# A recommender tower on one core: half-sums on GpSimd between gathers, transposes only when a stage is due

## The chip, the cores and the metric

One core of a Trainium2 chip runs the kernel. The metric is the device time in microseconds, lower is better. The core has a matrix engine (TensorE, PE in the profile), a vector engine (VectorE, DVE), an activation engine (ScalarE, ACT), a general one that here issues the gathers (GpSimd, POOL), and a queue engine for ordinary transfers (SyncE, SP). They work beside each other and meet only through semaphores.

## What is computed

All data are float32. For 2048 rows of a batch, 32 tables give one embedding of 64 numbers each; every pair of embeddings is combined through its own 64x64 matrix, and a small network follows:

```python
e = jnp.stack([tbl_0[ids[:, 0]], ..., tbl_31[ids[:, 31]]], axis=1)   # 2048 x 32 x 64
II, JJ = np.triu_indices(32, k=1)                                   # 496 pairs
z = jnp.sum(e, axis=-1)                                             # 2048 x 32
outer = jnp.einsum('bpd,pde,bpe->bp', e[:, II], kernels, e[:, JJ])  # 2048 x 496
h = jnp.concatenate([z, outer, dense_ctx], axis=1)                  # 2048 x 544
h = jnp.maximum(h @ W_top1 + b_top1, 0.0)                           # 512
h = jnp.maximum(h @ W_top2 + b_top2, 0.0)                           # 256
y = h @ W_top3                                                      # 1
```

## The kernel before

**Tiling.** The batch is cut into `NQ` = 4 quarters of `QB` = 512 rows, a quarter into 4 tiles of 128 rows. The 32 tables are taken in 16 pairs, the stages a = 0 to 15. A stage needs 8 gathers (4 tiles, 2 tables), each of 128 rows of 64 numbers into `gathered`, which has `GR` = 4 stage buffers. TensorE transposes a stage (`transpose`, line 322, four instructions into the one bank `tr`), and ScalarE copies it to `x_t` (`keep_x`, line 207), where the embeddings of two tables lie on 128 partitions with the batch along the row.

**Products.** The pair matrices stay in `k_sb`, loaded once in ten transfers, as 128 doubles; a double takes stage a against an earlier stage. Stage a brings a doubles, one more where a is odd, so the early stages bring few and the late ones many: the first double of stage a is number 0, 0, 2, 4, 8, 12, 18, 24, 32, 40, 50, 60, 72, 84, 98, 112 (`FIRST`). For each double TensorE makes two matmuls into one of `MR` = 3 pieces of `m_ps` (`multiply`, lines 386 and 387), VectorE multiplies 128x1024 results with `x_t` (`product`, line 300) into one of 7 buffers `prod`, and TensorE sums them over partitions with small selecting matrices into `acc` (`reduce`, line 398). Four doubles are a group g; a quarter has 32 groups, and the reduce of a group follows the products of the next. [...]

**Sums and layers.** The sum of each embedding is made by VectorE from `gathered` (`sum_x`, line 287, one reduction of 512 numbers to 8 for each partition and stage) into `z_nat`; TensorE turns it (piece "s"). The three layers of quarter q-1 (pieces "h1", four of them, "h2", two, and "y") are put between the groups of quarter q, after groups 1, 3, 5, 7, then 9, 11 and 13. Those of the last quarter stand at the end.

**The order** is written out by hand in two tables, `BEFORE` and `AFTER`, of what is done ahead of the products of a group and behind its reduce; all engines walk them in the same order (`ORDER`), since all pieces share the bank `tr`. In the first quarter stage a stands ahead of group `min(FIRST[a] // 4 - (a > 5), (4 a - 7) // 3)`, in later ones behind group 18 + 2a of the quarter before (`group_of_stage`, line 62), so that its transposes run on into group 16 of its own quarter.

**GpSimd** issues the 512 gathers in order (line 176), at most four in flight. The first gather of a stage waits for the transpose (`tr_filled`) and VectorE's sum (`x_summed`) of the stage four before it; in later quarters gather n of a stage also waits for VectorE's product 4 (g - 3) + n, g the group of its transpose, which spreads the gathers, one for each product:

```python
pool.wait_ge(prod_ready, GROUP * (group_of_stage(q, a) - 3) + n)
```

## Time and profile before

| | |
|---|---|
| median of 3 runs | 1015.3 us (1012.37 to 1015.33) |
| the profiled execution | 1018.13 us, its span 1016.3 us |
| mean granted clock of TensorE in it | 0.963 of full |
| TensorE busy | 886.5 us (87%) |
| VectorE busy | 641.3 us (63%) |
| GpSimd busy | 483.6 us (48%) |
| ScalarE busy | 69.3 us (7%) |

The profile is of one execution. Its busy times are unions of recorded spans; the ends of matmuls are modelled. A row of the timeline gives start, duration, engine, line, operation, what is written from what, and in brackets how long the engine sat idle before and who released it. "issue" is idle time with no releaser in the profile, "remote" one whose releaser is not recorded; some matmul records are missing.

### The profile page before, as it was taken

To read this page: it belongs to the slowest core of one execution; us is meant where nothing else is said; L and a number is where in the kernel's file an instruction comes from. 1 tells how busy PE (TensorE), PEld (TensorE's weight loads), DVE (VectorE), ACT (ScalarE), POOL (GpSimd) and SP (SyncE) were. 2 spreads that over 40 slices of the span, in tenths; PEclk is the share of its full clock that TensorE was granted. 3 is DMA by queue.
4 is the path that set the end of the run, shared out by engine and by line. 5 is a ranking of instruction groups with operands and counts; after the bars stand their busy time and mean duration, and the time that the engine had idled before them with its cause. 6 is when DMAs were issued, how large, how long until landed. Compare 5 with 4: busy or idle time off the path is not lost.

```text
span 1016.3 us, 11896 instructions
## 1 busy us (share of the span) xinstructions
PE 886.5 (87%) x4608; PEld 311.6 (31%) x4608; DVE 641.3 (63%) x579; ACT 69.3 (7%) x113; POOL 483.6 (48%) x518
## 2 busy tenths in 40 slices
PE   0323579699999999998999999998999999999998
PEld 0111123223333333333333333323333333333333
DVE  0102257578887575687877656676787657688850
ACT  0000000000000001000000101000000101000001
POOL 5774735536565444555666444554556445400000
PEclk9956779999999999999999999999999999999999
DMA  9310101101111000110111010011101000000000
GB/s 348 107 27 15 27 14 19 21 12 23 23 21 23 17 17 18 20 21 20 22 23 22 15 19 17 19 22 19 21 19 24 15 17 19 19 1 1 1 1 0
DMA packets 19777, 28.20 MB, mean 28 GB/s; under 512 B 8901, under 2 KB 9413, under 8 KB 18825
## 3 DMA queue, kind: packets, MB, share of 16 engines
q0 software_dynamic: 16384, 16.81, 8.6%
q1 hardware_dynamic: 3336, 10.63, 2.9%
q8 instruction: 37, 0.61, 0.3%
q14 instruction: 20, 0.16, 0.1%
HBM read 27.40 MB, written 0.01 MB: 27 GB/s over the span
## 4 chain that ended last, share of the span: by engine, by line
PE 77%; another core or an unknown queue 8%; issue 7%; DVE 4%; DMA 2%; ACT 1%; SPq 1%; POOL 1%; DVEq 0%; POOLq 0%
PE m_ps L386 39%; PE acc L398 21%; PE tr L341 4%; DVE prod L300 3%; PE tr L328 3%; PE tr L347 2%; PE m_ps L387 2%; DMA w_sb<-in_w 2%; PE m_ps L341 1%; PE tr L339 1%; PE m_ps L347 1%; PE tr L353 1%; POOL gathered L176 1%; SPq L186 1%
## 5 line engine op out<-in xcount | busy, mean ns | idle before, releaser
L300 DVE TENSOR_TENSOR prod<-m_ps,x_t 128x1024 f32<-128x1024 f32 x512 | 604.3, 1219 | 302.5 <-PE m_ps L387 180.7
L176 POOL DMA_INDIRECT gathered<-in_tbl,idx x512 | 482.9, 943 | 403.4 <-DVE prod L300 178.2
L386 PE MATMUL m_ps<-x_t,k_sb 64*128 64x512 f32 x1024 | 501.4, 623 | 74.6 <-DVE prod L300 35.6
L387 PE MATMUL m_ps<-x_t,k_sb 64*128 64x512 f32 x1024 | 502.3, 624 | 0.0
L386 PEld LDWEIGHTS m_ps<-x_t,k_sb 64*128 64x128 f32 x1024 | 180.7, 191 | 346.9 <-issue 261.6
L398 PE MATMUL acc<-prod,sel 128*32 128x512 f32 x2048 | 247.0, 600 | 0.0
L387 PEld LDWEIGHTS m_ps<-x_t,k_sb 64*128 64x128 f32 x1024 | 180.6, 191 | 0.0
L398 PEld LDWEIGHTS acc<-prod,sel 128*32 128x32 f32 x2048 | 53.7, 109 | 176.5 <-issue 119.6
L328 PE MATMUL tr<-ident,gathered 128*128 128x128 f32 x256 | 44.5, 299 | 50.6 <-DMA gathered<-in_tbl,idx 41.4
L213 ACT ACTIVATE x_t<-tr 128x512 f32<-128x512 f32 x64 | 38.2, 597 | 471.7 <-PE tr L328 275.3
L287 DVE TENSOR_REDUCE z_nat<-gathered 128x8 f32<-128x512 f32 x64 | 43.1, 675 | 38.1 <-DMA gathered<-in_tbl,idx 38.1
L328 PEld LDWEIGHTS tr<-ident,gathered 128*128 128x128 f32 x256 | 28.5, 147 | 100.7 <-issue 87.4
L341 PE MATMUL tr<-z_sb,w_sb 128*128 128x512 f32 x96 | 44.4, 605 | 0.0
L341 PEld LDWEIGHTS tr<-z_sb,w_sb 128*128 128x128 f32 x96 | 17.2, 189 | 26.3 <-issue 26.3
L247 ACT ACTIVATE z_sb<-acc 128x512 f32<-128x512 f32 x16 | 9.6, 597 | 202.4 <-PE acc L398 129.5
L347 PE MATMUL tr<-h_sb,w_sb 128*128 128x512 f32 x48 | 22.2, 605 | 0.0
L217 ACT ACTIVATE h_sb<-tr,b_sb 128x512 f32<-128x512 f32 x12 | 8.2, 687 | 112.3 <-PE tr L341 112.3
L341 PE MATMUL m_ps<-z_sb,w_sb 128*128 128x512 f32 x32 | 14.8, 605 | 0.0
L339 PE MATMUL tr<-z_sb,w_sb 48*128 48x512 f32 x24 | 13.5, 641 | 0.0
L347 PEld LDWEIGHTS tr<-h_sb,w_sb 128*128 128x128 f32 x48 | 8.6, 189 | 13.6 <-issue 13.6
L341 PEld LDWEIGHTS m_ps<-z_sb,w_sb 128*128 128x128 f32 x32 | 5.8, 189 | 8.8 <-issue 8.8
L353 PE MATMUL tr<-h_sb,w_sb 128*1 128x512 f32 x16 | 7.5, 592 | 0.8 <-ACT h_sb L268 0.8
(24 smaller groups left out, 39.6 us busy)
## 6 DMA issues: line engine op xcount, KB each, us to landing
gathered<-in_tbl,idx POOLq DMA_INDIRECT x512
k_sb<-in_kmat SPq DMA_DIRECT2D x7, 1024.0 KB, 14.3
w_sb<-in_w SPq DMA_DIRECT2D x1, 1280.0 KB
k_sb<-in_kmat SPq DMA_DIRECT2D x2, 256.0 KB, 4.2
k_sb<-in_kmat SPq DMA_DIRECT2D x1, 512.0 KB, 6.4
w_sb<-in_w SPq DMA_DIRECT2D x1, 512.0 KB
idx<-in_ids SPq DMA_DIRECT2D x1, 256.0 KB, 2.7
z_sb<-in_dense_t SPq DMA_DIRECT2D x4, 32.0 KB
```

Of the source, the lines that this page charges most:

```text
L176: nc.gpsimd.indirect_dma_start(out=gathered[:, G % GR, t, f, :], out_offset=None, in_=tables[2 * (STAGES - 1 - a) + f], in_offset=bass.Ind ...
L213: nc.scalar.activation(x_t[:, q % 2, a, :], tr[:], ACT.Copy).then_inc(tr_kept, 1)
L287: nc.vector.tensor_reduce(z_nat[:, q % 2, :, 2 * a:2 * a + 2], gathered[:, G % GR, :, :, :], axis=AX.X, op=ALU.add).then_inc(x_summed, 1)
L300: nc.vector.tensor_tensor(prod[:, p % PR, :, :], m_ps[:, p % MR, :, :], other, ALU.mult).then_inc(prod_ready, 1)
L328: last = nc.tensor.transpose(tr[:, t * P:(t + 1) * P], gathered[:, G % GR, t, :, :].rearrange("p f d -> p (f d)"), ident[:])
L339: nc.tensor.matmul(to, w1_sb[0:ZLAST, NB, n * P:(n + 1) * P], z_sb[0:ZLAST, NB, :], start=True, stop=False)
L341: last = nc.tensor.matmul(to, w1_sb[:, b, n * P:(n + 1) * P], z_sb[:, b, :], start=False, stop=(b == NB - 1))
L347: last = nc.tensor.matmul(to, w2_sb[:, c, n * P:(n + 1) * P], h1_sb[:, c, :], start=(c == 0), stop=(c == H1 // P - 1))
L353: last = nc.tensor.matmul(to, w3_sb[:, c:c + 1], h2_sb[:, c, :], start=(c == 0), stop=(c == H2 // P - 1))
L386: nc.tensor.matmul(m_ps[:, p % MR, 0, :], k_sb[0:D, d, :], x_t[0:D, q % 2, a0, :], start=True, stop=True)
L387: nc.tensor.matmul(m_ps[:, p % MR, 1, :], k_sb[D:P, d, :], x_t[D:P, q % 2, a1, :], start=True, stop=True).then_inc(unit_done, 1)
L398: last = nc.tensor.matmul(acc[c * 32:c * 32 + 32, :], sel[:, 30 - 2 * row:62 - 2 * row], prod[:, (q * ND + 2 * n + c // 2) % PR, c % 2, :] ...
```

## The change

GpSimd adds the two halves (32 and 32 numbers) of every gathered embedding into a new buffer `x_fold` of four stages: it is given 512 additions, each between two gathers, of the gather issued four earlier (`fold_x`). VectorE's reduction reads `x_fold`, 256 numbers for each partition, and has its own table `SUM_AT`: it stands where the next stage is due, that of stage 15 ahead of group 29. A gather no longer waits for a product; the first of a stage waits for the transpose four stages before, and the first addition of a stage waits for VectorE's sum four stages before. In the first quarter a stage stands ahead of group `FIRST[a] // 4 - (a > 8)`, in later ones behind the group just ahead of its first product, stages 0 and 1 behind groups 28 and 30 of the quarter before. The turned sums move to group 30. To make room in memory, `y_sb` becomes a part of `h2_sb`, and with it the wait for the store of y moves to the first eviction of h2.

```diff
--- before.py
+++ after.py
@@ -61,11 +61,11 @@
 
 def group_of_stage(q, a):
 
-    return 18 + 32 * (q - 1) + 2 * a
+    return min(NG * q - 4 + 2 * a, NG * q + FIRST[a] // GROUP - 1)
 
 
 for _a in range(STAGES):
-    _g = 0 if _a < 3 else min(FIRST[_a] // GROUP - (_a > 5), (4 * _a - 7) // 3)
+    _g = FIRST[_a] // GROUP - (_a > 8)
     BEFORE.setdefault((0, _g), []).append(("x", 0, _a))
 for _q in range(1, NQ):
     for _n in range(H1 // P):
@@ -75,8 +75,15 @@
     AFTER.setdefault((_q, 13), []).append(("y", _q - 1, 0))
     for _a in range(STAGES):
         AFTER.setdefault(divmod(group_of_stage(_q, _a), NG), []).append(("x", _q, _a))
-    AFTER.setdefault((_q, 18), []).append(("s", _q, 0))
-AFTER.setdefault((0, NG - 1), []).append(("s", 0, 0))
+    AFTER.setdefault((_q, 30), []).append(("s", _q, 0))
+AFTER.setdefault((0, 30), []).insert(0, ("s", 0, 0))
+
+
+SUM_AT = {}
+for _q in range(NQ):
+    for _a in range(STAGES):
+        _g = NG * _q + 29 if _a == STAGES - 1 else FIRST[_a + 1] // GROUP if _q == 0 else group_of_stage(_q, _a + 1) + 1
+        SUM_AT.setdefault(divmod(_g, NG), []).append((_q, _a))
 ORDER = [e for q in range(NQ) for g in range(NG) for e in BEFORE.get((q, g), []) + AFTER.get((q, g), [])]
 PLACE = {e: n for n, e in enumerate(ORDER)}
 
@@ -100,6 +107,7 @@
         k_sb = sb("k_sb", [P, ND, P])
         x_t = sb("x_t", [P, 2, STAGES, QB])
         gathered = sb("gathered", [P, GR, TILES, 2, D])
+        x_fold = sb("x_fold", [P, GR, TILES, 2, D // 2])
         prod = sb("prod", [P, PR, 2, QB])
         z_sb = sb("z_sb", [P, NB + 1, QB])
         z_nat = sb("z_nat", [P, 2, TILES, SUM_ROWS])
@@ -158,25 +167,32 @@
             nc.gpsimd.affine_select(out=ident[:], in_=ident[:], compare_op=ALU.not_equal, fill=1.0,
                                     base=0, pattern=[[-1, P]], channel_multiplier=1).then_inc(consts_ready, 1)
             pool.wait_ge(idx_loaded, 16)
-            for G in range(NQ * STAGES):
+            def fold_x(k):
+                G, n = divmod(k, GATHERS)
                 q, a = divmod(G, STAGES)
-                if G >= GR:
+                t, f = divmod(n, 2)
+                pool.wait_ge(gather_landed[k % IN_FLIGHT], (k // IN_FLIGHT + 1) * 16)
+                if n == 0 and G >= GR:
+                    pool.wait_ge(x_summed, G - GR + 1)
+                nc.gpsimd.tensor_tensor(x_fold[:, G % GR, t, f, :], gathered[:, G % GR, t, f, 0:D // 2],
+                                        gathered[:, G % GR, t, f, D // 2:D], ALU.add).then_inc(x_folded, 1)
+
+            for k in range(NQ * STAGES * GATHERS):
+                G, n = divmod(k, GATHERS)
+                q, a = divmod(G, STAGES)
+                t, f = divmod(n, 2)
+                if k >= IN_FLIGHT:
+                    fold_x(k - IN_FLIGHT)
+                if n == 0 and G >= GR:
                     pool.wait_ge(tr_filled, place("x", *divmod(G - GR, STAGES)))
-                    pool.wait_ge(x_summed, G - GR + 1)
-                for n in range(GATHERS):
-                    t, f = divmod(n, 2)
-                    if q:
-
-                        pool.wait_ge(prod_ready, GROUP * (group_of_stage(q, a) - 3) + n)
-                    k = G * GATHERS + n
-                    if k >= IN_FLIGHT:
-
-                        pool.wait_ge(gather_landed[k % IN_FLIGHT], k // IN_FLIGHT * 16)
-                    col = ((q * STAGES + a) * 2 + f) * TILES + t
-                    nc.gpsimd.indirect_dma_start(
-                        out=gathered[:, G % GR, t, f, :], out_offset=None, in_=tables[2 * (STAGES - 1 - a) + f],
-                        in_offset=bass.IndirectOffsetOnAxis(ap=idx[:, col:col + 1], axis=0),
-                    ).then_inc(gather_landed[k % IN_FLIGHT], 16)
+                    pool.wait_ge(x_folded, (G - GR + 1) * GATHERS)
+                col = ((q * STAGES + a) * 2 + f) * TILES + t
+                nc.gpsimd.indirect_dma_start(
+                    out=gathered[:, G % GR, t, f, :], out_offset=None, in_=tables[2 * (STAGES - 1 - a) + f],
+                    in_offset=bass.IndirectOffsetOnAxis(ap=idx[:, col:col + 1], axis=0),
+                ).then_inc(gather_landed[k % IN_FLIGHT], 16)
+            for k in range(NQ * STAGES * GATHERS - IN_FLIGHT, NQ * STAGES * GATHERS):
+                fold_x(k)
 
         @block.sync
         def _(sp):
...
@@ -218,13 +234,13 @@
 
             def keep_h2(q, n):
                 act.wait_ge(tr_filled, place("h2", q, n))
+                if q and n == 0:
+                    act.wait_ge(y_stored, 16 * q)
                 nc.scalar.activation(h2_sb[:, n, :], tr[:], ACT.Relu, bias=b2_sb[:, n:n + 1]).then_inc(tr_kept, 1)
 
             def keep_y(q):
                 act.wait_ge(tr_filled, place("y", q, 0))
-                if q:
-                    act.wait_ge(y_stored, 16 * q)
-                nc.scalar.activation(y_sb[:], tr[0:1, :], ACT.Copy).then_inc(tr_kept, 1)
+                nc.scalar.activation(y_sb, tr[0:1, :], ACT.Copy).then_inc(tr_kept, 1)
 
             def keep_sums(q):
                 act.wait_ge(tr_filled, place("s", q, 0))
...
@@ -277,16 +293,6 @@
             dve.wait_ge(sel_zeroed, 1)
             nc.vector.memset(sel[0:D, 30:31], 1.0).then_inc(consts_ready, 1)
             nc.vector.memset(sel[D:P, 31:32], 1.0).then_inc(consts_ready, 1)
-            def sum_x(q, a):
-                G = q * STAGES + a
-                for landed in gather_landed:
-                    dve.wait_ge(landed, (G + 1) * GATHERS // IN_FLIGHT * 16)
-                if q >= 2 and a == 0:
-
-                    dve.wait_ge(tr_filled, place("s", q - 2, 0))
-                nc.vector.tensor_reduce(z_nat[:, q % 2, :, 2 * a:2 * a + 2], gathered[:, G % GR, :, :, :],
-                                        axis=AX.X, op=ALU.add).then_inc(x_summed, 1)
-
             def product(q, d):
                 p, (_, _, u0, u1) = q * ND + d, DOUBLES[d]
                 dve.wait_ge(unit_done, p + 1)
@@ -299,16 +305,21 @@
                     other = x_t[:, q % 2, u0:u1 + 1, :]
                 nc.vector.tensor_tensor(prod[:, p % PR, :, :], m_ps[:, p % MR, :, :], other, ALU.mult).then_inc(prod_ready, 1)
 
+            def sum_x(q, a):
+                G = q * STAGES + a
+                dve.wait_ge(x_folded, (G + 1) * GATHERS)
+                if q >= 2 and a == 0:
+
+                    dve.wait_ge(tr_filled, place("s", q - 2, 0))
+                nc.vector.tensor_reduce(z_nat[:, q % 2, :, 2 * a:2 * a + 2], x_fold[:, G % GR, :, :, :],
+                                        axis=AX.X, op=ALU.add).then_inc(x_summed, 1)
+
             for q in range(NQ):
                 for g in range(NG):
-                    for what, h, n in BEFORE.get((q, g), ()):
-                        if what == "x":
-                            sum_x(h, n)
+                    for h, a in SUM_AT.get((q, g), ()):
+                        sum_x(h, a)
                     for d in range(GROUP * g, GROUP * (g + 1)):
                         product(q, d)
-                    for what, h, n in AFTER.get((q, g), ()):
-                        if what == "x":
-                            sum_x(h, n)
 
         @block.tensor
         def _(pe):
```

GpSimd in the second quarter. Ahead of the change, the gathers of a stage:

```order
L176 DMA gathered<-in_tbl,idx 128x64 [waits gather_landed3,prod_ready]
L176 DMA gathered<-in_tbl,idx 128x64 [waits prod_ready,gather_landed0,x_summed,tr_filled]
L176 DMA gathered<-in_tbl,idx 128x64 [waits gather_landed1,prod_ready]
L176 DMA gathered<-in_tbl,idx 128x64 [waits gather_landed2,prod_ready]
L176 DMA gathered<-in_tbl,idx 128x64 [waits gather_landed3,prod_ready]
```

and with it:

```order
L177 TENSOR_TENSOR x_fold<-gathered 128x32 [waits gather_landed0]
L190 DMA gathered<-in_tbl,idx 128x64 [waits x_folded,tr_filled]
L177 TENSOR_TENSOR x_fold<-gathered 128x32 [waits gather_landed1]
L190 DMA gathered<-in_tbl,idx 128x64
L177 TENSOR_TENSOR x_fold<-gathered 128x32 [waits gather_landed2]
L190 DMA gathered<-in_tbl,idx 128x64
L177 TENSOR_TENSOR x_fold<-gathered 128x32 [waits gather_landed3]
L190 DMA gathered<-in_tbl,idx 128x64
L177 TENSOR_TENSOR x_fold<-gathered 128x32 [waits x_summed,gather_landed0]
```

An addition stands ahead of each gather and holds the wait for the landing; the wait for a product is gone, and the one for VectorE's sum has moved four gathers on, to the stage's first addition.

TensorE in the first quarter, behind the reduce of group 1. Ahead of the change, stages 5 and 6 are transposed together ahead of group 3 (`tr` from `gathered`):

```order
L398 MATMUL acc<-prod,sel 32x512 x3
L328 MATMUL tr<-ident,gathered 128x128 [waits gather_landed3,gather_landed2,tr_kept,gather_landed1,gather_landed0]
L328 MATMUL tr<-ident,gathered 128x128 x3
L328 MATMUL tr<-ident,gathered 128x128 [waits gather_landed3,gather_landed2,tr_kept,gather_landed1,gather_landed0]
L328 MATMUL tr<-ident,gathered 128x128 x3
L386 MATMUL m_ps<-x_t,k_sb 128x512 [waits prod_ready,tr_kept,k_loaded2]
```

and with it, at the same place and behind the next reduce:

```order
L409 MATMUL acc<-prod,sel 32x512 x3
L339 MATMUL tr<-ident,gathered 128x128 [waits gather_landed3,gather_landed2,tr_kept,gather_landed1,gather_landed0]
L339 MATMUL tr<-ident,gathered 128x128 x3
L397 MATMUL m_ps<-x_t,k_sb 128x512 [waits prod_ready,tr_kept,k_loaded2]
```

Stage 6 has moved behind the four products of group 3, ahead of group 4, whose third product is its first.

VectorE in the first quarter. Ahead of the change (sums `z_nat`, products `prod`):

```order
L287 TENSOR_REDUCE z_nat<-gathered 128x4x2 [waits gather_landed2,gather_landed3,gather_landed1,gather_landed0] x2
L300 TENSOR_TENSOR prod<-m_ps,x_t 128x1024 [waits reduced,unit_done] x8
L287 TENSOR_REDUCE z_nat<-gathered 128x4x2 [waits gather_landed2,gather_landed3,gather_landed1,gather_landed0]
L300 TENSOR_TENSOR prod<-m_ps,x_t 128x1024 [waits reduced,unit_done] x8
```

and with it:

```order
L314 TENSOR_REDUCE z_nat<-x_fold 128x4x2 [waits x_folded]
L306 TENSOR_TENSOR prod<-m_ps,x_t 128x1024 [waits reduced,unit_done] x4
L314 TENSOR_REDUCE z_nat<-x_fold 128x4x2 [waits x_folded]
L306 TENSOR_TENSOR prod<-m_ps,x_t 128x1024 [waits reduced,unit_done] x8
```

A sum now waits for GpSimd's additions of its stage, and stands where the next stage's first product is due.

## Rows read from the trace of the kernel before

**Rows 1.** The page, busy us, share of the span, instructions of each engine.

```profile
PE 886.5 (87%) x4608; PEld 311.6 (31%) x4608; DVE 641.3 (63%) x579; ACT 69.3 (7%) x113; POOL 483.6 (48%) x518
```

**Rows 2.** Stretches of 25 us: busy time (and instructions) of each engine, clock, DMA.

```profile
core 0: us, PE busy (x) PEld busy (x) DVE busy (x) ACT busy (x) POOL busy (x), PEclk, DMA share, GB/s
50.00:75.00 25.00, 6.55 (x16) 2.75 (x16) 2.02 (x3) 0.60 (x1) 18.90 (x21) 0.52 0.14 27
...
100.00:125.00 25.00, 15.99 (x72) 5.46 (x68) 8.10 (x8) 1.19 (x2) 18.74 (x21) 0.77 0.13 26
125.00:150.00 25.00, 16.58 (x76) 5.52 (x76) 13.00 (x12) 0.60 (x1) 9.21 (x11) 0.73 0.07 14
150.00:175.00 25.00, 22.26 (x130) 7.58 (x132) 19.57 (x18) 1.68 (x3) 12.92 (x14) 1.00 0.10 19
...
500.00:525.00 25.00, 23.97 (x140) 8.01 (x136) 19.88 (x19) 1.79 (x3) 15.08 (x16) 1.00 0.12 22
```

**Rows 3.** The chain that ended last, in order of time: start, duration, what.

```profile
334.29 3.63 PE tr L341 x8
...
557.78 3.63 PE tr L341 x8
...
785.53 3.63 PE tr L341 x8
...
936.49 1.85 PE acc L398 x16
941.98 1.85 PE acc L398 x16
...
980.40 3.62 PE acc L398 x32
```

**Rows 4.** Groups of instructions: form and count, busy us and mean ns, idle before.

```profile
L328 PE MATMUL tr<-ident,gathered 128*128 128x128 f32 x256 | 44.5, 299 | 50.6 <-DMA gathered<-in_tbl,idx 41.4 <-ACT x_t L213 4.8 <-ACT z_sb L231 4.5
L287 DVE TENSOR_REDUCE z_nat<-gathered 128x8 f32<-128x512 f32 x64 | 43.1, 675 | 38.1 <-DMA gathered<-in_tbl,idx 38.1
```

**Rows 5.** Timeline of GpSimd at the start: start us, duration us, instruction.

```profile
0.25 0.10 POOL L470 MEMSET const-float32-0.0<- 128x1 f32 x1 [0.25 <-issue]
...
1.19 0.28 POOL L158 TENSOR_SCALAR_AFFINE_SELECT ident<-ident 128x128 f32<-128x128 f32 x1 [0.24 <-POOL ident L156]
3.73 1.10 POOL L176 DMA_INDIRECT gathered<-in_tbl,idx  x1 [2.26 <-DMA idx<-in_ids]
...
38.11 0.94 POOL L176 DMA_INDIRECT gathered<-in_tbl,idx  x1 [0.30 <-issue]
```

**Rows 6.** Timeline of the first quarter, 41 to 98 us, all engines.

```profile
41.74 1.22 PE L386 MATMUL m_ps<-x_t,k_sb 64*128 64x512 f32 x1
...
50.67 1.09 PE L328 MATMUL tr<-ident,gathered 128*128 128x128 f32 x4 [2.85 <-DMA gathered<-in_tbl,idx]
...
67.88 0.60 ACT L213 ACTIVATE x_t<-tr 128x512 f32<-128x512 f32 x1 [25.43 <-issue]
...
68.57 1.19 PE L386 MATMUL m_ps<-x_t,k_sb 64*128 64x512 f32 x1 [16.81 <-issue]
...
79.78 1.23 DVE L300 TENSOR_TENSOR prod<-m_ps,x_t 128x1024 f32<-128x1024 f32 x1 [21.28 <-remote]
...
88.04 0.94 POOL L176 DMA_INDIRECT gathered<-in_tbl,idx  x1 [0.30 <-issue]
...
96.84 0.60 ACT L213 ACTIVATE x_t<-tr 128x512 f32<-128x512 f32 x1 [28.37 <-remote]
```

**Rows 7.** Timeline, two later ends of unbroken gathers and what followed.

```profile
128.46 0.94 POOL L176 DMA_INDIRECT gathered<-in_tbl,idx  x1 [0.30 <-issue]
...
133.56 4.71 DVE L300 TENSOR_TENSOR prod<-m_ps,x_t 128x1024 f32<-128x1024 f32 x4 [4.54 <-remote]
...
165.26 0.94 POOL L176 DMA_INDIRECT gathered<-in_tbl,idx  x1 [0.30 <-issue]
...
167.96 1.23 DVE L300 TENSOR_TENSOR prod<-m_ps,x_t 128x1024 f32<-128x1024 f32 x1 [2.46 <-remote]
```

11 lines of the change are left out of this document (6 added, 5 removed).

## The prediction

> **What bounds the kernel now.** I read the busy times first [rows 1]: TensorE is busy for 886.5 us of a span of 1016.3 us (87%), VectorE for 641.3, GpSimd for 483.6. So some 130 us of the span are not TensorE's, and the question is where they lie. The table by stretches [rows 2] answers it: in the stretches from 50, 100 and 125 us TensorE is busy 6.55, 15.99 and 16.58 us of 25, and its granted clock is 0.52 to 0.77; from 500 us it is busy 23.97 of 25 at full clock. The tail after the last reduce, which ends at 984 [rows 3], is the layers of the last quarter, and this change leaves it alone.
>
> Where TensorE is full, a group of four products costs 5.49 us: two reduces in the chain of work stand at 936.49 and 941.98 [rows 3]. A quarter of the batch is 32 groups, 175.7 us; its 16 transposes add 11 (44.5 us for 64 of them, 0.70 each [rows 4]), its layers 27: eight matmul records of L341 take 3.63 [rows 3], a layer-1 part has ten, so 4.54, and there are four; two layer-2 parts have eight, and layer 3 four, 1.8. That is 214 us. The first layer-1 matmuls of successive quarters stand at 334.29, 557.78 and 785.53 [rows 3], 223 and 228 us apart: later quarters lie only 9 to 14 us over their floor. The first one starts its products at 41.7 us [rows 6] and should need 32 groups (176), 19 transposes (13) and two more groups (11), so layer 1 could start at about 242; it starts at 334. **Ninety us are lost in the first quarter**, and they are what this change can win.
>
> Why are they lost? GpSimd issues a gather every 1.25 us there: 0.94 busy and 0.30 in front [rows 5, 6]. A stage is eight gathers, 10 us, so the gathers of 16 stages could be done by 4 + 160 = 164 us, and for the first five groups TensorE does wait for data. But the timeline [rows 6] shows something else as well. The transpose of stage 3 ran at 50.67 to 51.76, and ScalarE, with nothing else to do, evicted it only at 67.88. Products that TensorE started at 68.57 were taken by VectorE at 79.78. What TensorE signals arrives late, while what ScalarE and VectorE signal is acted on at once (67.88 + 0.60 is followed by TensorE at 68.57). It is released when GpSimd pauses: the gathers stop at 88.98, and ScalarE goes on at 96.84; they stop at 129.40, and VectorE is free at 133.56; in a short burst they stop at 166.20, and VectorE goes on at 167.96 [rows 6, 7]. Over the lengths of these bursts (56, 30 and 10 us) the arrears of 7.9, 4.2 and, less a usual 0.3, 1.4 us are all near 14%. So I take it that a gather in an unbroken row leaves 1.25 x 1.14 = 1.42 us of something that delays TensorE's signals, and that nothing piles up when gathers stand 1.42 us apart or more. In later quarters, where a gather waits for each product, they come 16 in 25 us, 1.6 us apart [rows 2], and TensorE is full. This is an inference; its cause in the hardware I cannot name.
>
> **The change part by part.** *The fold on GpSimd*: 512 additions of 128x32. No row shows one. The nearest are the affine select of 128x128 at 0.28 us, with 0.24 us of idle time in front, and a set of 128x1 at 0.10 us [rows 5]. Lower bound 0.10 with no gap of its own (cadence 1.35), upper bound 0.28 plus a gap of 0.30 (cadence 1.83). I take 0.17 plus 0.08, nearer to the 128x1 row since a fold has 32 elements for each partition, so a gather every **1.50 us**; it waits for no landing, since the gather it reads was issued four gathers (6 us) earlier, and in the trace of before, where four gathers are 5.0 us, the idle time is the plain 0.30 [rows 5, 6]. On GpSimd this adds 512 x 0.25 = 128 us to 484 busy, on an engine idle for over half the span: it is hidden, except where gathers are the bound.
>
> The Trainium skill (GPSIMD Engine Reference, Performance versus the Vector engine) says that a two-input elementwise instruction on GpSimd costs about 2.6 cycles for each element and speaks against putting it there; for 32 elements that would be an estimate of 0.07 us beyond the dispatch. No run here shows it, and by it alone the cadence would stay near 1.4 and the time near the lower end of my range.
>
> *Start-up*: TensorE's first product needs stage 2, 24 gathers. The first starts at 3.73 and the 24th at 38.11 [rows 5], 1.49 us apart on average, since some are held by landings while the loads run; 20 folds at 0.25 put it 5 us later at most, so products start at 45 instead of 41.7.
>
> *The first quarter's new order*: a stage is transposed one group or less before its first product; stages 5 and 6 are no longer both wanted in group 3, and stages 10 to 15 are wanted in groups 11, 14, 17, 20, 23 and 27 instead of 11, 12, 13, 15, 16 and 17. With 8 x 1.50 + 0.2 = 12.2 us for a stage, stage a is there at 45 + 12.2 x (a - 2): stage 6 at 94, stage 8 at 118, stage 10 at 143, stage 15 at 204. If TensorE's signals are prompt, it waits for stages 3 to 10 (groups 0 to 10), and from group 11 it is the bound: 21 groups at 5.49 are 115, nine transposes and one set of sums 7, so the first quarter ends at 143 + 122 = 265 and layer 1 begins two groups later, at 277. While it waits TensorE is busy for about half the time, so the granted clock will be at its lower level as from 50 us now [rows 2]; a group at 1.2 GHz, some 10 us (2.4 GHz gives 5.49), is still under the 12.2 of a stage, but groups 4 to 10 lose some; I add 3 to 6. Layer 1 at 282 to 283 against 334.29: **minus 51 us**.
>
> *VectorE's sums*: the reduction reads 256 elements for each partition instead of 512. It took 0.675 us for 512 [rows 4]; a product of 1024 takes 1.23 [rows 6], so an element is near 1 ns, and it saves about 0.27 us x 64 = 17 us of VectorE, which is not the bound (4 x 1.23 of 5.49 us in a group). Where the sum delays a product that TensorE waits for, some of it is won: minus 0 to 8, I take 4.
>
> *No pacing in later quarters*: a gather no longer waits for a product. It is held by four buffers: gather 0 of a stage by the transpose four stages back, and the fold in front of gather 4 by VectorE's sum four stages back. So a stage comes as four and four, or eight in a row, and then a pause. *Stages wanted close together*: at a quarter's end stages 2 to 6 are transposed after groups 31 to 35. From the moment when VectorE has summed stage 15 (group 29), 24 gathers lie between it and the landing of stage 5, 32 for stage 6. In time, groups 29 to 34 last 5.5, 6.8, 6.1, 6.1, 10.7 (with a layer-1 part) and 6.1: stage 5 is wanted 41 us after it, stage 6 52 us after. Gathers at 1.50 bring them at 36 + 2.1 and 48 + 2.1, just in time; at 1.83, at 46 and 61, so 5 and then 4 us late, three times. I take plus 2 for each of three ends: plus 6. The other edits (sums after group 30, y written over h2, waits for the store of y that ended a quarter before) have time behind other work: nothing, and if the store were late, 2 us of ScalarE.
>
> Sum: -51 - 4 + 6 = **-49 us**. From the profiled execution, 1018.1 us (span 1016.3), that gives 969; the median of the runs shown is 1015.3, and so **966 us**.
>
> **The rivals.** *TensorE's signals stay late.* For it: the folds may not thin out what delays them (if the 1.42 us is work of GpSimd's own, a fold adds to it, and 1.42 + 0.17 is more than 1.50), and the pauses of the later quarters are gone. The first quarter would then crawl as now, in runs of gathers ended by the four buffers: gain 0 to 20. The later quarters would look like 142 to 200 us now, where bursts of eight end with a signal 1.8 us late at 166 and TensorE lacks 2.7 us of 25 [rows 2, 7]; 48 stages at 1.2 to 1.5 us are 58 to 72. Time: 1015 - 20 + 50 = **1045**, between 1015 and 1075. It decides from a cadence under the 1.42 us, or a rate of arrears that grows with the fold. Against it: 1.6 us apart there is no trace of it.
>
> *The fold is dear (cadence 1.8 or more).* Stage 15 would come at 48 + 13 x 14.8 = 240, the first quarter would end at 295 (gain 24), and three ends would cost 9 each: 1015 - 24 + 27 = **1018**, no change.
>
> *The waits of the first quarter cost more*: TensorE cold until group 14 and stages at 13.5 us each: layer 1 at 300, **985 to 1000**.
>
> *Better than the sum*: cadence 1.38 and prompt signals let stage 10 come at 133, and the later quarters come nearer to their floor: 1015 - 61 - 15 = **940 to 950**.
>
> **How the numbers follow.** My sum, with a cadence of 1.42 to 1.65 (950 to 982): 0.52. Costly waits (983 to 1000): 0.12. Better than 950: 0.09. Dear fold (about 1018): 0.07, of which 0.04 is within 0.3% (1012 to 1018, about what a measurement of this kernel can tell from no change) and 0.03 slower. Late signals: 0.20, of which 0.02 faster, 0.02 the same and 0.16 slower. So faster 0.75, same 0.06, slower 0.19. The range leaves out most of the part under 950 and the upper half of the late signals: 948 to 1042.
>
> **What would show it.** GpSimd's gathers in the first 100 us 1.4 to 1.6 us apart and the fold 0.10 to 0.28 us; ScalarE's eviction of each transpose within 1 us of it; layer 1 of the first quarter at 275 to 295; TensorE 24 to 25 us busy in each 25 from 200 us on, also at the ends of quarters. Wrong: evictions 5 us or more after their transposes while gathers run, gathers over 1.8 us apart, or TensorE at 20 to 22 in 25 all through.

## The result, and the profile after

The changed kernel takes 1073.45 us (median of 3 runs, 1072.43 to 1076.22) where the kernel before takes 1015.3: 1.059 times as long, 95% interval 1.055 to 1.063. The forecast was 966 us and faster, so it was wrong in sign; the rival "TensorE's signals stay late" (1015 to 1075) is the one whose range holds it. The profiled execution has a span of 1070.6 us, against 1016.3.

One fact that the first two traces did not hold has to be told first, since everything after it rests on it. The experiments ran on five chips, and the same kernel before takes 931 to 935 us on three of them and 1010 to 1022 us on the other two. (Three of its runs are slow ones and left out: 1510 us at a granted clock of 0.57, 1105 us at 0.83, and one of 1026 us.) I call them **kind A** (934 us) and **kind B** (1015 us). The prediction and the result are of kind B. None of the five chips served for more than one set of experiments, so whether the kind belongs to the chip or to the hour is not shown; "chip" below means the set that ran on it. The changed kernel is slower on both: 1.036 times (1.034 to 1.038) on kind A.

The page's first part, busy times of the changed kernel, beside [rows 1]:

```profile
PE 895.0 (84%) x4608; PEld 320.6 (30%) x4608; DVE 626.4 (59%) x579; ACT 70.2 (7%) x113; POOL 626.6 (59%) x1030
```

TensorE is now idle for 176 us of the span, before for 130. VectorE has lost 15 us of work and GpSimd has won 143, but neither bounds the kernel. The stretches of 25 us of the changed kernel, columns as in [rows 2]:

```profile
50.00:75.00 25.00, 14.56 (x56) 6.38 (x56) 8.80 (x10) 1.19 (x2) 21.95 (x36) 0.73 0.12 24
100.00:125.00 25.00, 7.89 (x30) 2.02 (x32) 5.23 (x5) 0.60 (x1) 21.82 (x36) 0.59 0.12 24
275.00:300.00 25.00, 17.45 (x92) 6.56 (x86) 10.08 (x10) 1.18 (x2) 21.19 (x35) 0.86 0.13 24
325.00:350.00 25.00, 14.09 (x56) 5.33 (x49) 6.78 (x7) 1.28 (x2) 21.81 (x36) 0.80 0.12 24
550.00:575.00 25.00, 16.54 (x66) 6.44 (x60) 7.45 (x8) 2.48 (x4) 21.84 (x37) 0.87 0.12 24
800.00:825.00 25.00, 17.74 (x60) 6.91 (x62) 7.67 (x7) 2.48 (x4) 21.83 (x36) 0.80 0.12 24
```

From 50 us TensorE is busy for twice the time that it was before (14.56 against 6.55 of 25), from 100 us for half of it (7.89 against 15.99): the first quarter is better in parts only. New are the holes at the ends of the quarters, at 275, 325, 550 and 800 us, where TensorE falls to 14 to 18 of 25 and its clock to 0.80 to 0.87. In every one of them GpSimd is busy for 21 to 22 of 25, which means gathers and folds without a break.

The first matmul of layer 1 of each quarter but the last (it answers to [rows 3]) shows how the 54 us between the two spans are spread. Timeline of TensorE in the changed kernel (start us, duration us; x2 are the two records that the trace has of this one matmul, as it has 1024 at one line for its 512 products):

```profile
313.06 1.12 PE L350 MATMUL tr<-z_sb,w_sb 48*128 48x512 f32 x2
...
562.04 1.12 PE L350 MATMUL tr<-z_sb,w_sb 48*128 48x512 f32 x2
...
809.85 1.12 PE L350 MATMUL tr<-z_sb,w_sb 48*128 48x512 f32 x2
```

I use the same instruction as a mark in all kernels. The table gives where it first stands, the two distances to the next ones, and the rest to the end of the span, in us, from each kernel's own timeline:

| kernel (kind of chip) | first mark | quarter | quarter | rest | span |
|---|---|---|---|---|---|
| before (B) | 333.2 | 223.5 | 227.7 | 231.9 | 1016.3 |
| changed (B) | 313.1 | 249.0 | 247.8 | 260.7 | 1070.6 |
| e5 before (A) | 272.9 | 214.1 | 214.1 | 231.7 | 932.7 |
| e6 changed (A) | 266.7 | 226.3 | 226.3 | 245.8 | 965.2 |
| e1 no gathers in quarters 2 to 4 (A) | 268.4 | 225.9 | 225.9 | 245.5 | 965.7 |
| e8 new order alone (A) | 257.3 | 226.3 | 226.3 | 245.7 | 955.7 |
| e2 every fold twice (A) | 293.3 | 237.5 | 226.3 | 245.8 | 1002.9 |
| e7 one group earlier (A) | 265.7 | 221.8 | 215.8 | 235.5 | 938.7 |
| e14 folds alone (A) | 288.5 | 214.1 | 214.1 | 231.9 | 948.5 |
| e16 first quarter's order alone (A) | 257.2 | 230.6 | 214.1 | 231.7 | 933.6 |
| e18 folds alone (B) | 320.5 | 219.5 | 219.4 | 232.0 | 991.3 |
| e9 first quarter's order alone (B) | 348.9 | 267.1 | 225.3 | 232.3 | 1073.6 |
| e11 new order one group earlier (B) | 356.7 | 249.8 | 252.9 | 248.7 | 1108.0 |
| e12 no spacing of gathers (B) | 370.1 | 237.0 | 235.5 | 231.7 | 1074.3 |
| e10 layers moved (B) | 314.2 | 244.4 | 232.4 | 255.0 | 1046.0 |
| e17 one group earlier, spaced (B) | 330.4 | 240.4 | 245.8 | 235.9 | 1052.5 |

The rows of kind B come from different chips, and these differ by some us: the kernel before has a median of 1015.3, 1014.5 and 1018.6 us on three of them, and only the first has its trace. A difference of two B rows holds to some us only.

The changed kernel on kind B: 20 us won before the first mark, then 25.5, 20.1 and 28.8 lost. The kernel before is itself not at its best there: its three later parts take 683.1 us, and 659.9 on kind A. The floor of 214 us that the prediction worked out for a quarter is what kind A measures (214.1).

What the prediction said of single instructions can be read in the groups and in GpSimd's timeline of the changed kernel:

```profile
L177 POOL TENSOR_TENSOR x_fold<-gathered 128x32 f32<-128x32 f32 x512 | 134.1, 262 | 242.0 <-DVE z_nat L314 227.6
L314 DVE TENSOR_REDUCE z_nat<-x_fold 128x8 f32<-128x256 f32 x64 | 26.2, 409 | 32.9 <-POOL x_fold L177 32.9
```
```profile
40.19 0.96 POOL L190 DMA_INDIRECT gathered<-in_tbl,idx  x1 [0.16 <-issue]
41.17 0.26 POOL L177 TENSOR_TENSOR x_fold<-gathered 128x32 f32<-128x32 f32 x1
41.59 0.96 POOL L190 DMA_INDIRECT gathered<-in_tbl,idx  x1 [0.16 <-issue]
```

The fold's row shows a new brake, too: GpSimd stands for 227.6 us for VectorE's sums, which come one stage late by the new order, and then gathers in a row again. A fold takes 0.26 us, and gathers stand 1.40 us apart (41.59 - 40.19), not 1.50; the sum takes 0.41 us, not 0.675 [rows 4].

### The profile page after: what moved, and what is told of

Its sections match the earlier page's. It is cut to its first block, busy times and chain, and to the rows that moved or that the text cites. A ratio compares the mean times of both kernels' runs of the same rounds, so it can differ in the third digit from the quotient of the medians.

```text
span 1070.6 us, 11958 instructions
## 1 busy us (share of the span) xinstructions
PE 895.0 (84%) x4608; PEld 320.6 (30%) x4608; DVE 626.4 (59%) x579; ACT 70.2 (7%) x113; POOL 626.6 (59%) x1030
## 4 chain that ended last, share of the span: by engine, by line
PE 66%; another core or an unknown queue 14%; issue 6%; DMA 5%; POOL 3%; ACT 3%; DVE 2%; DVEq 0%; POOLq 0%
PE m_ps L397 38%; PE acc L409 19%; DMA gathered<-in_tbl,idx 4%; PE tr L339 3%; POOL gathered L190 2%; PE tr L358 2%; DVE prod L306 2%; ACT x_t L229 2%; PE m_ps L352 1%; PE m_ps L398 1%; POOL x_fold L177 1%; PE m_ps L358 1%; PE tr L364 1%; PE m_ps L350 0%
## 5 line engine op out<-in xcount | busy, mean ns | idle before, releaser
L397 PE MATMUL m_ps<-x_t,k_sb 64*128 64x512 f32 x1024 | 507.1, 635 | 88.7 <-issue 39.9
L190 POOL DMA_INDIRECT gathered<-in_tbl,idx x512 | 491.9, 961 | 94.2 <-issue 87.5
L398 PE MATMUL m_ps<-x_t,k_sb 64*128 64x512 f32 x1024 | 507.4, 635 | 0.0
L397 PEld LDWEIGHTS m_ps<-x_t,k_sb 64*128 64x128 f32 x1024 | 189.7, 197 | 360.3 <-issue 257.2
L177 POOL TENSOR_TENSOR x_fold<-gathered 128x32 f32<-128x32 f32 x512 | 134.1, 262 | 242.0 <-DVE z_nat L314 227.6
L398 PEld LDWEIGHTS m_ps<-x_t,k_sb 64*128 64x128 f32 x1024 | 189.2, 197 | 0.0
L314 DVE TENSOR_REDUCE z_nat<-x_fold 128x8 f32<-128x256 f32 x64 | 26.2, 409 | 32.9 <-POOL x_fold L177 32.9
L233 ACT ACTIVATE h_sb<-tr,b_sb 128x512 f32<-128x512 f32 x12 | 8.2, 687 | 182.2 <-PE tr L352 125.6
L350 PE MATMUL tr<-z_sb,w_sb 48*128 48x512 f32 x24 | 13.5, 641 | 0.0
L239 ACT ACTIVATE h_sb<-tr,b_sb 128x512 f32<-128x512 f32 x6 | 4.1, 687 | 69.8 <-PE tr L358 69.8
```

What stands on the lines that cost most here:

```text
L177: nc.gpsimd.tensor_tensor(x_fold[:, G % GR, t, f, :], gathered[:, G % GR, t, f, 0:D // 2], gathered[:, G % GR, t, f, D // 2:D], ALU.add).t ...
L190: nc.gpsimd.indirect_dma_start(out=gathered[:, G % GR, t, f, :], out_offset=None, in_=tables[2 * (STAGES - 1 - a) + f], in_offset=bass.Ind ...
L314: nc.vector.tensor_reduce(z_nat[:, q % 2, :, 2 * a:2 * a + 2], x_fold[:, G % GR, :, :, :], axis=AX.X, op=ALU.add).then_inc(x_summed, 1)
L350: nc.tensor.matmul(to, w1_sb[0:ZLAST, NB, n * P:(n + 1) * P], z_sb[0:ZLAST, NB, :], start=True, stop=False)
L397: nc.tensor.matmul(m_ps[:, p % MR, 0, :], k_sb[0:D, d, :], x_t[0:D, q % 2, a0, :], start=True, stop=True)
L398: nc.tensor.matmul(m_ps[:, p % MR, 1, :], k_sb[D:P, d, :], x_t[D:P, q % 2, a1, :], start=True, stop=True).then_inc(unit_done, 1)
```

## Where the signals are late, and where they are not

On kind B the late signals of [rows 6] are still there at 1.40 us. TensorE and ScalarE in the changed kernel's first quarter:

```profile
65.19 0.63 PE L339 MATMUL tr<-ident,gathered 128*128 128x128 f32 x4 [1.75 <-DMA gathered<-in_tbl,idx]
77.08 0.66 PE L339 MATMUL tr<-ident,gathered 128*128 128x128 f32 x4
...
94.18 0.66 PE L339 MATMUL tr<-ident,gathered 128*128 128x128 f32 x4
```
```profile
68.98 0.60 ACT L229 ACTIVATE x_t<-tr 128x512 f32<-128x512 f32 x1 [13.16 <-remote]
86.12 0.60 ACT L229 ACTIVATE x_t<-tr 128x512 f32<-128x512 f32 x1 [16.54 <-remote]
...
112.96 0.60 ACT L229 ACTIVATE x_t<-tr 128x512 f32<-128x512 f32 x1 [26.25 <-remote]
```

The transposes end at 65.82, 77.74 and 94.84, and ScalarE, idle meanwhile, copies them 3.2, 8.4 and 18.1 us later. The last is longer than the 16.1 us of the kernel before [rows 6], at the wider gap, in a row of 67 gathers that ends only at 124. In the hole at 550 us the same thing, with a piece of layer 1:

```profile
563.09 3.70 PE L352 MATMUL tr<-z_sb,w_sb 128*128 128x512 f32 x8
...
569.96 0.69 ACT L233 ACTIVATE h_sb<-tr,b_sb 128x512 f32<-128x512 f32 x1 [15.11 <-remote]
...
570.79 0.63 PE L339 MATMUL tr<-ident,gathered 128*128 128x128 f32 x4 [4.00 <-ACT h_sb L233]
```

The piece ends at 566.79, its copy starts 3.2 us later, and TensorE, which wants to write a transpose into the same bank, stands for 4.00 us. Now the same place of the same kernel on kind A (e6):

```profile
494.11 3.70 PE L352 MATMUL tr<-z_sb,w_sb 128*128 128x512 f32 x8
...
498.68 0.63 PE L339 MATMUL tr<-ident,gathered 128*128 128x128 f32 x4 [0.87 <-ACT h_sb L233]
```
```profile
497.85 0.69 ACT L233 ACTIVATE h_sb<-tr,b_sb 128x512 f32<-128x512 f32 x1 [10.33 <-PE tr L352]
```

It ends at 497.81 and is copied at 497.85. And the kernel before on kind A (e5), first quarter, gathers 1.25 us apart without a break as in [rows 6]:

```profile
50.81 1.09 PE L328 MATMUL tr<-ident,gathered 128*128 128x128 f32 x4 [4.29 <-DMA gathered<-in_tbl,idx]
```
```profile
51.93 0.60 ACT L213 ACTIVATE x_t<-tr 128x512 f32<-128x512 f32 x1 [9.46 <-PE tr L328]
```

0.03 us after the transpose's end, where kind B took 16 us [rows 6]. A gather takes the same time on both (944 and 943 ns on average).

All traces can be counted this way. ScalarE makes 90 copies from `tr` in each kernel. In every one of the twelve traces of kind A one of the 90 starts over 0.6 us after the end of TensorE's last instruction into `tr`, and it is the first of all (at 28 us). In the eight traces of kind B it is 22 to 35 of the 90. Those of the kernel before are not all in its first quarter: 27 of its 35 come after 240 us, 0.8 to 3.0 us late, where the gathers are paced. There they stand 1.8 us apart on average, yet still in short bursts: behind 334 us 197 of its 307 gaps are under 1.3 us. One of the 27, behind gathers at 676.60, 677.85, 679.10, 680.35, 682.45, 683.88 and 685.12:

```profile
685.15 0.61 PE L335 MATMUL tr<-ident,z_nat 128*32 128x128 f32 x4
...
687.47 0.59 ACT L231 ACTIVATE z_sb<-tr 32x512 f32<-32x512 f32 x1 [13.09 <-remote]
```

So the late signals go with the kind of chip and with gathers, not with one kernel; what differs in those chips no run here tells. Nor can a trace tell a signal that travels late from matmuls that end later than their modelled end. The Trainium skill (Perfetto Trace Analysis, Per-instruction lifecycle) says that the propagation of a semaphore lies outside the window that the profiler reports. The traces agree in so far as the 16 us are part of no instruction and appear only as idle time of the engine that waits.

## The experiments

In the diffs, lines are cut to what changes. The kernel before ran beside each set of experiments on the same chip: 933.8 us (e1 to e4), 933.3 (e5 to e8), 1014.5 (e9 to e12), 933.2 (e13 to e16), 1018.6 (e17 and e18). The theories: **late signals** (TensorE's signals come late in unbroken gathers), **supply** (rows come too late), and **placement** (a stage turned right before its first product costs TensorE, gathers or not).

### No gathers in quarters 2 to 4 (e1, e15)

```
+ if q == 0:
      nc.gpsimd.indirect_dma_start(...)
```
(and the waits for a landing stand only in the first quarter; the folds stay in all four)

> The changed kernel without the gathers of quarters 2 to 4 (their folds, sums, transposes and products stay, on the rows of the first quarter, so the output is not the reference's). Three theories of the loss at the quarter ends (275 to 375 us, 550 to 625 us, 800 to 850 us of the changed kernel). Late signals: TensorE's signals come 3 to 10 us late while gathers run unbroken, so without gathers each of the three quarters that follow takes about 240 us, the y evictions stand 238 to 241 us apart and the kernel takes 985 to 1000 us. Supply: the rows come too late; without them the same 985 to 1000 us, but then a run whose gathers come less often must be slower, not faster. Placement: TensorE waits for ScalarE's copy before each stage and for the layer pieces in the shared bank; then the time stays near 1060 us without any gather, with windows of 17 to 21 us of TensorE at the quarter ends.

Measured on kind A: 967.2 us, 1.036 times the kernel before (1.034 to 1.037). The same kernel with all its gathers takes 966.92 there (e6). So on kind A the gathers and the arrival of rows cost nothing after the first quarter, and the loss of 33 us is **placement** (in e6's row of the table 38.7 after the first mark, less 6.2 won before it); supply falls. The folds, which stay in e1, cost nothing in those quarters either: e3 below has them in the old order, at 214.1 us a quarter. It is neither of the numbers that I had given: the theories of a loss by gathers put the time at 985 to 1000 because they were worked out from kind B. e15, the same kernel again, fell on kind A too and gave 966.42:

> The changed kernel without the gathers of quarters 2 to 4 (its output is not the reference's), once more, for a chip on which the kernel before takes 1015 us. If the gathers are all that such a chip does worse: the three quarters that follow take 226 us each as on the other chips, the time is the first quarter's 289 us more than on those, 1000 to 1015 us in all. If the chip is slower in something else: quarters of 235 us or more without any gather, 1030 us or more.

What the changed kernel would take on kind B without gathers stays unmeasured.

### Every fold twice (e2, e13)

```
  nc.gpsimd.tensor_tensor(x_fold..., gathered..., ALU.add).then_inc(folded_once, 1)
+ pool.wait_ge(folded_once, k + 1)
+ nc.gpsimd.tensor_tensor(x_fold..., gathered..., ALU.add).then_inc(x_folded, 1)
```


> The changed kernel with every fold done twice, which widens the gap of two gathers from 1.40 to about 1.85 us. Late signals: at 1.85 us GpSimd leaves the signals through (as with the 1.9 us pacing of the kernel before), so the quarter ends come back and the time falls to 1000 to 1030 us; a stage every 14.8 us is still enough for most stages. Supply: a stage takes 14.8 instead of 11.2 us, the first quarter and each quarter end lose more, 1100 to 1150 us. Placement: no change outside the first quarter, 1075 to 1090 us.

Measured on kind A: 1004.6 us (1.076), gathers 1.71 us apart. The time falls in the range of "late signals", but for another reason: there are no late signals on this chip. The first mark is at 293.3 (266.7 with single folds) and the next distance 237.5 (226.3); after that 226.3 and 245.8, the same as with single folds. So rows bind mainly until the first boundary, and there the gap counts: ScalarE's copy of stage 10 comes at 159.4 us instead of 133.2, and from there to the mark the distance stays at 26 us. Eleven stages (0 to 10) of eight gathers, each 0.31 us wider, come to 27. The repetition fell on kind A as well (1003.7 us):

> The changed kernel with every fold done twice (gap of two gathers about 1.85 us), once more, for a chip on which the kernel before takes 1015 us. On a chip where it takes 934 us this kernel took 1004.6 us. Late signals, let through by a wider gap: the slow chip gives the same 1000 to 1020 us here, less than the changed kernel's 1073 us. Late signals, whatever the gap: 1070 to 1110 us. On a chip of 934 us: 1004 us again, and nothing new.

### The folds alone (e3, e14, e18)

The kernel before, with its order and its spacing; only the halves are added on GpSimd between gathers and the sums read `x_fold` (`y_sb` stays a part of `h2_sb`).

> The kernel before with its order and its pacing of the gathers, and only the folds on GpSimd with shorter sums on VectorE. Late signals: pacing keeps the signals prompt in quarters 2 to 4 and the folds widen the gap in quarter 1, 985 to 1010 us. Fold is dear: GpSimd's extra 0.4 us for each gather delays rows, 1020 to 1040 us. If the fold gives nothing and costs nothing: 1010 to 1018 us.

Kind A: 950.4 us, 1.018 (1.016 to 1.020). The table shows where: first mark 288.5 against 272.9, then 214.1, 214.1 and 231.9, which is the kernel before to 0.2 us. "Fold is dear" had the mechanism: 0.15 us a gather, 1.2 us a stage, and the first quarter is bound by the arrival of rows where the signals are prompt. A shorter sum on VectorE is worth nothing there. e14 (kind A) repeated it, 950.1:

> The order and the pacing of the kernel before with the folds on GpSimd, once more, for a chip on which the kernel before takes 1015 us (on one of 934 us it took 950 us). If the folds' wider gap is what mends the first quarter on the slow chip (turned sums at 290 us in the changed kernel with folds, 335 to 357 us in three kernels without): 980 to 1000 us there, faster than both kernels. If it is the new order of the first quarter: 1010 us or more.

> The order and the pacing of the kernel before with the folds on GpSimd, a last time, for a chip on which the kernel before takes 1015 us (two chips of 933 us gave 950 us, 1.018 times the kernel before). If the gap of 1.40 us in place of 1.25 us is what mends the first quarter there: 980 to 1000 us. If not: 1010 us or more. On a chip of 933 us: 950 us again, and nothing new.

Kind B at last: **987.0 us against 1018.6, 0.969 times (0.966 to 0.972)**, faster than both kernels. The first mark comes 12.7 us earlier than before, and each quarter takes 219.5 us instead of 223.5 and 227.7 (traces of two chips; and the profiled execution, 993.1, is the longest of its four, so the gains are at the small end). The edit that costs 17 us on kind A gives 32 on kind B. Whether it is the gap of 1.40 us or the addition between two gathers that lets signals through is not separated. They are not all let through: 28 of the 90 copies are over 0.6 us late, the longest by 8.3 us. From 100 us:

```profile
100.00:125.00 25.00, 7.92 (x30) 2.38 (x32) 3.67 (x3) 0.00 (x0) 21.80 (x37) 0.59 0.12 24
```

which is as bad as the changed kernel's row from 100 us (7.89). Of the 20.1 us that the changed kernel won before the first mark, the folds alone give 12.7. The new order adds 7.4 to them, of which some 3 are transposes that only moved behind the mark (e8, below), and without folds it lost 16 us there (e9).

### Three stages of the first quarter one group later (e4)

```
-    _g = 0 if _a < 3 else min(FIRST[_a] // GROUP - (_a > 5), (4 * _a - 7) // 3)
+    _g = 0 if _a < 3 else min(FIRST[_a] // GROUP - (_a > 8), (4 * _a - 7) // 3)
```


> The kernel before with the transposes of stages 6, 7 and 8 of the first quarter one group later (4, 6 and 8 instead of 3, 5 and 7), nothing else. If the first quarter's gain in the changed kernel comes from not stopping TensorE for a stage before it is due: 5 to 12 us faster, 1003 to 1010 us. If the first quarter is bound by the arrival of the rows and the late signals alone: 1013 to 1017 us.

934.5 against 933.8 us, ratio 1.0007 (0.9997 to 1.0017): nothing on kind A. Both figures expected were for kind B, where it was not run.

### Both kernels on kind A (e5, e6)

> The kernel before, word for word, to have its trace on this chip: on the chip of the runs so far it took 934 us, on the first one 1015 us. Late signals depend on the chip: here TensorE's transposes of 40 to 100 us reach ScalarE within 1.5 us, and every window of 25 us from 175 us on is 24 to 25 us of TensorE. If the difference is another one (slower matmuls, a lower clock), the quarters themselves are longer on the slow chip, with dense windows on both.

934.2 us, and from 100 us on TensorE is 25.00 of 25 in all stretches but a few. Two rows of e5:

```profile
50.00:75.00 25.00, 16.33 (x76) 6.82 (x76) 11.58 (x11) 1.79 (x3) 18.91 (x21) 0.79 0.13 27
...
500.00:525.00 25.00, 25.00 (x116) 8.93 (x114) 13.62 (x13) 1.97 (x3) 11.86 (x13) 1.00 0.10 19
```

16.33 us of TensorE from 50 us where kind B has 6.55 [rows 2], beside the same 18.9 us of gathers.

> The changed kernel, word for word, on a chip where the kernel before takes 934 us. Placement costs about 12 us for each of three quarters here as without gathers, so 36 us. Late signals: if they also appear here at a gap of 1.40 us, the three quarter ends lose another 15 to 25 us each and the time is 1010 to 1040 us; if this chip lets the signals through, the time is that without gathers, 965 to 980 us.

966.9 us (1.036). The second half of what was expected holds: on this chip the time is that without gathers. Its stretch from 500 us, with GpSimd as full as in the holes of kind B and TensorE 7 us fuller:

```profile
500.00:525.00 25.00, 23.44 (x120) 8.74 (x122) 14.79 (x14) 1.88 (x3) 21.82 (x37) 1.00 0.13 24
```

The 12.3 us by which each of two quarters is longer than before (226.3 against 214.1) stand in its waits. Waits of e6 in one quarter, 374 to 600 us, TensorE's own (total us, times, longest):

```profile
PE m_ps L397 <- ACT x_t L229: 6.2, 9, 0.7
...
PE tr L339 <- ACT h_sb L233: 3.5, 4, 0.9
...
PE tr L339 <- ACT h_sb L239: 1.7, 2, 0.9
...
PE tr L339 <- ACT z_sb L247: 0.8, 1, 0.8
```

Together 12.2, where e5 has 0.8 in a quarter (its one wait for the copy of the sums): 11.4 of the 12.3 us. Nine stages are transposed with nothing between them and their first product, so TensorE waits 0.7 us for ScalarE's copy; six transposes follow a piece of a layer in the one bank `tr` and wait 0.9 us for that copy. This is placement, priced.

### One group earlier (e7), and with spaced gathers (e17)

```
-    return min(NG * q - 4 + 2 * a, NG * q + FIRST[a] // GROUP - 1)
+    return min(NG * q - 4 + 2 * a, NG * q + FIRST[a] // GROUP - 1) - 1
```


> The changed kernel with the transposes of quarters 2 to 4 one group earlier than the changed kernel has them, so each stage has a group between its transpose and its first product, and no transpose stands beside a piece of a layer except one. Placement: the wait for ScalarE's copy before a stage and the wait for the shared bank go, 10 to 12 us for each of three quarters, 25 to 35 us less than the changed kernel in the same call. Supply: each stage is due 7.7 us earlier with the same four buffers, so the time stays or grows by up to 20 us. Late signals alone: within 5 us of the changed kernel.

Kind A: 942.6 us, 24 less than the changed kernel, still 1.010 times the kernel before (1.009 to 1.012). In 370 to 586 us only three of TensorE's waits on ScalarE are left:

```profile
PE tr L339 <- ACT h_sb L233: 0.9, 1, 0.9
PE tr L339 <- ACT h_sb L243: 0.8, 1, 0.8
PE tr L339 <- ACT z_sb L247: 0.8, 1, 0.8
```

2.5 us instead of 12.2, and the quarter takes 215.8 instead of 226.3, which is 1.7 over e5 as are its waits (2.5 against 0.8). Placement is shown by this pair. e17 is this kernel with `if q: pool.wait_ge(prod_ready, GROUP * (group_of_stage(q, a) - 4) + n)` in front of each fold and gather:

> The changed kernel with its transposes of quarters 2 to 4 one group earlier and with a wait that spaces the gathers of these quarters, one for each product, from four groups before the stage is transposed. Without the wait this took 942.6 us on a chip on which the kernel before takes 933 us. Late signals: on a chip of 1015 us the spacing gives most of the quarter ends back, 980 to 1015 us, no slower than the kernel before. If spacing is worth nothing there: 1030 to 1060 us. On a chip of 933 us: 940 to 945 us, as without the wait; above 950 us if the wait makes rows come late.

Kind B: 1060.8 us, 1.045 times the kernel before (1.039 to 1.051): not the 980 to 1015 that spacing should have given. What it is worth is not measured, since the same kernel without the wait did not run on kind B; the changed kernel has 1.059. GpSimd does wait for products in e17, 51 times and for 194 us in all, but not in the holes. The reason is in the order. Stages 2 to 6 are due one group after another, a group is 5.5 to 7 us, and a stage's gathers with folds take 8 x 1.40 = 11.2, so by this count the waits are passed as soon as they are reached. GpSimd's timeline of e17 in the hole at 525 us (TensorE 14.98 of 25):

```profile
530.10 0.96 POOL L192 DMA_INDIRECT gathered<-in_tbl,idx  x1 [0.16 <-issue]
531.07 0.27 POOL L177 TENSOR_TENSOR x_fold<-gathered 128x32 f32<-128x32 f32 x1
531.50 0.96 POOL L192 DMA_INDIRECT gathered<-in_tbl,idx  x1 [0.16 <-issue]
```

1.40 us apart, as without a wait; 32 gathers stand in this row, and the copies in it are up to 8.2 us late. **With these late places and four buffers, a quarter's end is a burst of gathers by itself.**

### The new order alone (e8), and one group earlier (e11)

```
-    return 18 + 32 * (q - 1) + 2 * a
+    return min(NG * q - 4 + 2 * a, NG * q + FIRST[a] // GROUP - 1)
...
-    _g = 0 if _a < 3 else min(FIRST[_a] // GROUP - (_a > 5), (4 * _a - 7) // 3)
+    _g = FIRST[_a] // GROUP - (_a > 8)
...
-                    if q:
-                        pool.wait_ge(prod_ready, GROUP * (group_of_stage(q, a) - 3) + n)
```
(and the turned sums behind group 31, where the changed kernel has them behind 30; e11 has `- 1` behind the new `min(...)`, as e7)

> The kernel before with the new places of the transposes and of the turned sums, without folds, and without the wait that spaces the gathers: gathers follow each other at 1.25 us. Placement: the same 12 us for each of three quarters, 965 to 975 us where the kernel before takes 934 us. Late signals: at 1.25 us they are worse than at 1.40 us, so slower than the changed kernel, by 10 to 60 us. If the folds were the cost of the changed kernel, this one is within 1% of the kernel before.

Kind A: 957.5 us (1.026, 1.024 to 1.028), 9.4 less than the changed kernel, all of it before the first mark (257.3 against 266.7): the folds' price. I expected 965 to 975; the quarters cost 12.2 and 12.2 and the rest 14.0 as expected, but the first mark comes 15.6 us early. Some 3 us of that are four transposes of quarter 2 that now stand behind the mark; the rest is won: TensorE no longer stops for the rows of stages that it doesn't need yet (it is busy for 19.20 us from 150 to 175 us in e5 and for 25.00 in e8).

> The new order one group earlier in quarters 2 to 4, no folds, no pacing wait. The folds cost 9.4 us (957.5 against 966.9 us) and the group in between gives 24 us, so 930 to 936 us beside 934. If the folds are worth something once the placement is mended: no less than the changed kernel with the group in between, 941 to 945 us. Late signals: on a chip that shows them, slower than the kernel before by 3% or more, since the gathers follow each other at 1.25 us.

Kind B: 1109.2 us, 1.090 (1.082 to 1.099), the slowest of all: gathers at 1.25 us, in bursts, at every quarter's end, where copies come up to 9.4, 10.6 and 12.3 us late. What it would take on kind A was not measured. "Late signals" expected 3% or more.

### The first quarter's places alone (e9, e16)

```
-    _g = 0 if _a < 3 else min(FIRST[_a] // GROUP - (_a > 5), (4 * _a - 7) // 3)
+    _g = FIRST[_a] // GROUP - (_a > 8)
...
+    if q == 1:
+        return min(28 + 3 * a // 2, NG + FIRST[a] // GROUP - 1)
     return 18 + 32 * (q - 1) + 2 * a
```


> The kernel before with the changed kernel's places for the transposes of the first quarter alone (no folds, the pacing of the later quarters kept); quarter 2's stages go behind groups 28 to 50, quarters 3 and 4 as before. In the changed order without folds the turned sums of quarter 1, behind the same group 31, stood at 243.7 us instead of 261.4. If the first quarter's part of the change is its gain and the later quarters' part its loss: 17 us faster where the kernel before takes 934 us, 915 to 922 us. If quarter 2's early stages then wait for rows, half of it goes: 922 to 928 us. If late placement costs everywhere: 930 to 940 us.

> The kernel before with the changed kernel's places in the first quarter alone, once more, for a chip on which the kernel before takes 934 us (on one of 1015 us it took 1076 us). If the places of the first quarter are a gain where the signals come in time: 915 to 925 us beside 934, faster than both kernels there. If not: 930 to 940 us. On a chip of 1015 us: 1076 us again, and nothing new.

e9 met kind B: 1076.2 us (1.058, 1.050 to 1.066), and e16 kind A: 935.8 (1.003, 1.002 to 1.004). Both miss what I expected of a gain. On kind A the 15.7 us at the first mark are given back by the next (230.6 against 214.1): quarter 2, whose first stages can't be turned before quarter 1's last, takes on four transposes (2.8 us), 6.7 us of waits for ScalarE at its crowded places, and 5.9 us of waits for rows. TensorE's waits of e16 from 257 to 488 us:

```profile
PE tr L330 <- DMA gathered<-in_tbl,idx: 5.9, 4, 3.3
PE m_ps L388 <- ACT x_t L215: 3.4, 5, 0.7
PE tr L330 <- ACT h_sb L219: 2.6, 3, 0.9
```

On kind B the first mark is at 348.9, 16 us later than in the trace of before: without folds the new order does not help the first quarter there.

### The layers on other groups (e10)

```
-    AFTER.setdefault((_q, 1 + 2 * _n), []).append(("h1", _q - 1, _n))
+    AFTER.setdefault((_q, (1, 2, 4, 6)[_n]), []).append(("h1", _q - 1, _n))
...
-    AFTER.setdefault((_q, 9 + 2 * _n), []).append(("h2", _q - 1, _n))
+    AFTER.setdefault((_q, 8 + 2 * _n), []).append(("h2", _q - 1, _n))
```
(and `y` behind group 12 instead of 13)

> The changed kernel with the pieces of the layers behind groups 1, 2, 4, 6, 8, 10 and 12 of a quarter instead of 1, 3, 5, 7, 9, 11 and 13, so that five of seven no longer stand beside a transpose in the one bank. If the shared bank is 5.4 us of the 12.3 us that placement costs in a quarter (waits for ScalarE's copy before a transpose), four fifths of it go: 9 to 14 us less than the changed kernel, 952 to 958 us beside 967. If only the wait before a stage's first product costs: 964 to 968 us.

Kind B: 1050.7 us, 1.032 times the kernel before (1.024 to 1.040), where the changed kernel has 1.059. I expected 9 to 14 us less (on kind A) and it is 23 (between two kind B chips, so to some us). A likely reason is that on kind B a wait for ScalarE's copy in the shared bank costs up to 5.5 us in the changed kernel (4.00 above) and not 0.9; no run separates it.

### No spacing of the gathers (e12)

```
-                    if q:
-                        pool.wait_ge(prod_ready, GROUP * (group_of_stage(q, a) - 3) + n)
```


> The kernel before without the wait that spaces the gathers of quarters 2 to 4. Late signals: on a chip like the first one the quarters that are dense at an hour glance lose 20 us or more each, 1050 to 1090 us; on a chip that lets the signals through the spacing is worth nothing, within 0.3% of the kernel before. If bursts of gathers cost by themselves (descriptors or the memory port), it is slower by over 1% on any chip.

Kind B: 1072.7 us, 1.053 times the kernel before (1.045 to 1.061), one wait less and 58 us more on the same chip: as slow as the changed kernel. The spacing that I took for incidental is what keeps the kernel before at 1015 there. By the marks 37 us of it fall ahead of the first, 13.5 and 7.8 in the two quarters and none behind; I had expected 20 or more in each. From 200 us, where quarter 2's gathers now stand beside quarter 1's products:

```profile
200.00:225.00 25.00, 12.27 (x36) 3.35 (x36) 8.38 (x7) 0.16 (x1) 12.28 (x13) 0.58 0.09 18
```

This edit was not run on kind A; e8, which has it too, shows no burst there that costs anything beyond placement (226.3 us a quarter, and 225.9 without any gathers in e1).

## Why the prediction was wrong, point by point

- **Gap and fold.** Right in kind, 1.40 us instead of 1.50; the bounds 1.35 to 1.83 held it. The estimate of 0.07 us beyond the dispatch, from a figure of the Trainium skill (GPSIMD Engine Reference, Performance versus the Vector engine), had led to a gap near 1.4 and came closer than the row that I chose. The trace gives 0.26 us for a whole fold and does not part it into dispatch and work.
- **"Nothing piles up at 1.42 us or more"**. The step that failed, and with it the term "minus 51". It was drawn from three bursts of one trace. At the 1.40 us that came, its own rule leaves 0.02 us a gather, about 1 us over the 45 gathers from 31.8 to 94.8 us; measured are 3.2, 8.4 and then 18.1 us. So the rule fails by its size where it could be tested; no run on kind B has gathers in a row further apart than 1.40. The first quarter gained 20.1 us instead of 51: 12.7 by the folds alone (e18), and some 3 of the rest only transposes moved behind the mark.
- **"Plus 6" for the quarter ends**. Sized by rows in time alone, and the greatest miss. Measured 25.5 + 20.1 + 28.8 = 74.4 us, and -20.1 + 74.4 is the loss of 54 between the spans. Kind A has 12.3, 12.3 and 14.1, together 38.7: placement, which is there without a gather. The other 36 arise on kind B alone, where copies at the ends of the quarters come 3 to 7 us late. The split takes placement to cost the same on both kinds, which was not measured.
- **"The other edits: nothing"**. The placement term was missing. I followed the transposes' due times for the rows and not for TensorE's own wait on ScalarE: nine waits of 0.7 us and seven of 0.9 in a quarter. It could have been read: a copy takes 0.60 us, and the change puts it between a transpose and its product.
- **No pacing**. I had asked what the removed wait costs in rows, and found nothing. Its removal costs the kernel before 58 us on kind B (e12), and in the new order it does not reach the holes even where it is put back (e17).
- **VectorE's sums, -4**: 0.41 us as worked out, and worth 0.0 in a quarter on kind A (214.1 with and without); on kind B not separated.
- **The rival "signals stay late"** named the late signals from the rows at 142 to 200 us, with a time of 1045, to 1075, and I gave it 0.20. Its range held 1073 partly by luck: it put 58 to 72 us on late signals in the later quarters (of which its sum took 50), and of the 74.4 measured about half is placement, which it did not have. Against it I had held that 1.6 us apart there is no trace of late signals. That was misread: 1.6 is an average over bursts, 27 copies there are 0.8 to 3.0 us late, and TensorE's 23.97 of 25, which I called full, is 25.00 on kind A. The kernel before loses 23 us to it in its three later parts (683.1 against 659.9).
- **A slip in the sum**: 277 plus 3 to 6 is 280 to 283, not 282 to 283; it does not matter beside the rest.

The path from here: of the two parts of the change, the folds alone beat both kernels on kind B (0.969), and the new order loses on both kinds (e8 on A; e11, one group earlier, on B). On kind A none of these kernels beats the kernel before.

## What to carry to other kernels

A step that is moved to "only when due" has to be paid for from its result backwards: count every hop between it and its user (here transpose, copy by another engine, product), and leave one unit of other work between. Late places also decide when buffers come free, so they turn a steady stream of gathers into bursts; a wait that looks idle may be what keeps that stream spaced. An average over a stretch (16 gathers in 25 us) does not say that they are evenly spaced. And a threshold drawn from three points of one trace belongs into the rivals, not into the sum.

## What the runs showed of the hardware

- The same kernel takes 931 to 935 us on three chips and 1010 to 1022 us on others, with the same durations of gathers (0.94 us) and products (1.22 us). What the traces show to differ is when ScalarE and VectorE go on after TensorE while GpSimd gathers: 0.03 us after the end, or 16 us (same transpose, same gap of 1.25 us). On kind B one addition between the gathers (1.40 us) leaves up to 18.1 us of it.
- An edit can have opposite signs on two chips: the folds give 1.018 on kind A and 0.969 on kind B. A verdict from one chip says little of another, and comparisons here are made on one chip.
- A GpSimd addition of 128x32 between two gathers takes 0.26 us and widens the gap by 0.15 us only (1.25 to 1.40), since half of the idle 0.30 us in front of a gather goes with it; a second one, with a wait for the first, adds 0.31 (1.71). VectorE's product takes 1.22 us beside it as without.
